# V stored channel by unit, units innermost, in an attention and feed-forward block on one Trainium2 core

## The reference, cut to what matters

```
n = layernorm(x)
q, k, v = n @ Wq, n @ Wk, n @ Wv             # 16 heads of 64 channels
M, Z = memory0, z0                           # per sequence and head
for each segment of 128 rows:                # 4 segments
    att_dot = softmax(mask(q k^T / 8)) @ v
    sq, sk = elu(q) + 1, elu(k) + 1
    att_mem = (sq @ M) / (sq @ Z^T)
    M, Z = M + sk^T @ v, Z + sum(sk)
    out = (gate * att_mem + (1 - gate) * att_dot) @ Wo
x = x + layernorm(out)
x = x + layernorm(ffn(layernorm(x)))         # ffn: three cycles of a small four-layer net
```

## Time and profile before

| | |
|---|---|
| median of three runs | 1286.04 us |
| the profiled execution | 1285.42 us, its span 1283.6 us, mean TensorE clock 0.946 of full |
| TensorE matmuls busy | 1092.2 us, 85% |
| weight loads busy | 761.9 us, 59% |
| VectorE | 876.0 us, 68% |
| ScalarE | 594.8 us, 46% |
| GpSimd | 581.6 us, 45% |
| chain that ended last | TensorE 49%, VectorE 30%, issue 11%, ScalarE 6% |
| 96 stream transposes of `take_x` (L771) | 190.4 us, 7% of the span on the chain |

### The profile page before, as it was taken

One profiled execution on the slowest core, in us unless ns is written; L12 is line 12 of the kernel. 1 busy time (PEld: TensorE's weight loads), 2 busy tenths in 40 slices (PEclk: granted clock), 3 DMA queues, 4 the chain that ended last, 5 costly groups with the idle time before them and its releaser, 6 DMA issues.

```text
span 1283.6 us, 20628 instructions
## 1 busy us (share of the span) xinstructions
PE 1092.2 (85%) x7108; PEld 761.9 (59%) x7172; DVE 876.0 (68%) x1540; ACT 594.8 (46%) x1255; POOL 581.6 (45%) x715
## 2 busy tenths in 40 slices
PE   2798989896989898878889888898989779999992
PEld 1475767664757676657676766576767665433431
DVE  4868686866686868666868686868686654443486
ACT  4354444444454445543535454444444543444453
POOL 2145454544354545444545454545454552222264
PEclk9999999988999989989999999999999888999995
DMA  5000000000000000000000000000000010300033
GB/s 160 21 10 9 10 9 10 10 13 7 10 9 10 9 9 9 9 11 10 9 9 9 9 9 9 9 9 9 9 1 9 2 27 1 139 0 0 1 65 66
DMA packets 14682, 24.02 MB, mean 19 GB/s; under 512 B 5104, under 2 KB 6896, under 8 KB 14064
## 3 DMA queue, kind: packets, MB, share of 16 engines
q1 hardware_dynamic: 14576, 22.63, 5.8%
HBM read 13.97 MB, written 8.65 MB: 18 GB/s over the span
## 4 chain that ended last, share of the span: by engine, by line
PE 49%; DVE 30%; issue 11%; ACT 6%; POOL 2%; DMA 1%; SPq 0%; DVEq 0%; POOLq 0%; ACTq 0%
PE ps L1068 11%; PE ps L1173 9%; DVE arena L771 7%; PE ps L1279 6%; PE ps L1126 5%; DVE arena L868 3%; PE ps L1292 3%; PE ps L1131 3%; PE ps L1113 2%; ACT arena L557 2%; DVE arena L715 2%; DVE arena L781 2%; DVE arena L802 2%; PE ps L1158 2%; DVE arena L785 2%
## 5 line engine op out<-in xcount | busy, mean ns | idle before, releaser
L1068 PE MATMUL ps<-arena 128*128 128x512 f16 x1152 | 273.6, 389 | 6.0 <-DVE arena L747 4.2
L557 ACT ACTIVATE arena<-ps,arena 128x128 f32<-128x128 f32 x512 | 138.9, 383 | 223.5 <-DVE arena L792 223.2
L771 DVE STREAM_TRANSPOSE arena<-ps 128x1024 f32<-128x1024 f32 x96 | 190.4, 1985 | 43.3 <-PE ps L1068 43.3
L1068 PEld LDWEIGHTS ps<-arena 128*128 128x128 f16 x1152 | 113.7, 100 | 131.5 <-issue 17.9
L402 POOL TENSOR_TENSOR arena<-arena 128x256 f32<-128x256 f32 x128 | 92.9, 726 | 164.0 <-DVE arena L802 164.0
L1126 PEld LDWEIGHTS ps<-arena 128*128 128x128 f32 x1024 | 134.2, 200 | 25.2 <-issue 16.9
L1126 PE MATMUL ps<-arena 128*128 128x65 f32 x1024 | 136.8, 278 | 12.9 <-DVE arena L802 11.6
L386 POOL TENSOR_TENSOR arena<-arena 128x512 f32<-128x512 f32 x64 | 81.3, 1270 | 124.6 <-ACT arena L550 124.6
L1173 PE MATMUL ps<-arena 128*128 128x256 f32 x544 | 122.0, 382 | 0.3 <-ACT arena L569 0.3
L1173 PEld LDWEIGHTS ps<-arena 128*128 128x128 f32 x544 | 102.0, 190 | 16.0 <-issue 0.8
L372 POOL TENSOR_TENSOR arena<-arena 128x2 f32<-128x2 f32 x50 | 9.7, 195 | 218.2 <-DVE arena L711 218.2
(11 more groups left out here) (109 smaller groups left out, 1937.8 us busy)
## 6 DMA issues: line engine op xcount, KB each, us to landing
x_rows<-arena SPq DMA_DIRECT2D x17, 256.0 KB, 2.0
arena<-in_L_attn_x_dram SPq DMA_DIRECT2D x64, 64.0 KB
arena<-x_rows SPq DMA_DIRECT2D x4, 1024.0 KB, 7.9
out_dram<-arena SPq DMA_DIRECT2D x32, 128.0 KB, 2.9
arena<-in_L_attn_Wq_dram SPq DMA_DIRECT2D x1, 1024.0 KB, 12.9
arena<-in_L_attn_Wk_dram SPq DMA_DIRECT2D x1, 1024.0 KB, 15.0
arena<-in_L_attn_Wv_dram SPq DMA_DIRECT2D x1, 1024.0 KB, 17.1
arena<-in_L_attn_Wo_dram SPq DMA_DIRECT2D x1, 1024.0 KB, 13.0
```

Source lines behind the costliest of these rows:

```text
L557: last = act.activation(Pr[:, par, j, :], s_bank[:, par, j * P:(j + 1) * P], ACT.Exp, bias=negm[:, par, j:j + 1])
L771: dve.transpose(dst[:, d0:d0 + 32, :], bank.rearrange("p w (d c) -> p d w c", c=C)).then_inc(x_free, 1)
L1068: last = pe.matmul(bank[:, w, :], xc[:, lx, k, w * P:(w + 1) * P], W16[lw][:, k, i, :], start=(n == 0), stop=(n == 5))
```

## The change

V loses its padding and is stored with the channel as the slow index: word `e * 32 + u` in place of `u * 68 + e`. The ones become 32 adjacent words at the end. All users of V follow.

```diff
-VS = DK + 4
...
-        v_pos = [alloc(UNITS * VS)]
+        v_pos = [alloc(UNITS * DV1)]
...
-        v_pos.append(alloc(UNITS * VS))
+        v_pos.append(alloc(UNITS * DV1))
...
-                pool.memset(v_pos[0].rearrange("p (u e) -> p u e", u=UNITS)[:, :, DK:DV1], 1.0).then_inc(init, 1)
+                pool.memset(v_pos[0][:, DK * UNITS:], 1.0).then_inc(init, 1)
...
-                pool.memset(v_pos[1].rearrange("p (u e) -> p u e", u=UNITS)[:, :, DK:DV1], 1.0).then_inc(init, 1)
+                pool.memset(v_pos[1][:, DK * UNITS:], 1.0).then_inc(init, 1)
...
-                    dst = (q_pos, k_pos, v_pos)[i // 2][par].rearrange("p (u e) -> p e u", u=UNITS)
+                    dst = (q_pos, k_pos, v_pos)[i // 2][par].rearrange(
+                        "p (e u) -> p e u" if i >= 4 else "p (u e) -> p e u", u=UNITS)
...
                 def read_out(bp, s, g, half):
...
-                    v = v_pos[s % 2].rearrange("p (u e) -> p u e", u=UNITS)
+                    v = v_pos[s % 2].rearrange("p (e u) -> p u e", u=UNITS)
...
                 def remember(bp, s, g):   (TensorE's)
...
-                    v = v_pos[s % 2].rearrange("p (u e) -> p u e", u=UNITS)
+                    v = v_pos[s % 2].rearrange("p (e u) -> p u e", u=UNITS)
```

## The result

The changed kernel takes 1297.33 us (median of four runs, 1296.86 to 1299.14) against 1286.23 us for the kernel before: ratio 1.0089, 95% interval 1.0076 to 1.0103. It is 11 us slower where no change was forecast. The time lies inside the stated range of 1271 to 1320, but outside the 1280 to 1292 that the forecast's own case allowed. The profiled execution has a span of 1295.4 us.

The account below looks back on a forecast made before the run. The prediction took the TensorE-VectorE hand-offs as the bound, TensorE being fuller. 1285.42 - 12.3 (transposes) + 12 (stepping reads) = 1285.1, with 0.6 for the median 1285.7 us; stated range 1271 to 1320.

Parts of the forecast that it names:

- the forecast's own case: Whole kernel: transposes' gain and TensorE's cost nearly cancel, 1285.7 us, own range 1280 to 1292, chance 0.48.
- U0b: Second half of remember(0), before read_out(1, 1): taken as hidden while VectorE is late, within 0.05 us a step.
- U1: remember(1), after read_out(1, 1): taken as hidden while VectorE is late, within the same 0.05 us a step.
- The gain: V's transposes in take_x (L771): 0.82 us saved each, one a step on the chain, 12.3 us.
- ScalarE's slow rate: TensorE's stepping read of V, given ScalarE's rate for a stepping read: about 1.7 ns a column.
- Rival 1: TensorE's matmuls on V: the step is hidden altogether, only the gain stands, 1274 us; chance 0.27.
- rival 3: TensorE's matmuls on V: every column is fetched twice, some 1445 us; chance 0.06.
- rival 4: V's transposes don't get faster while TensorE pays as in the forecast, 1298 us; chance 0.07.
- rival 2: TensorE's matmuls on V: the step costs more and TensorE becomes the bound, 1315 us; chance 0.12.
- U2b: Second half of remember(2): on the chain with the read-out behind it, 0.40 us, 4.0 us in all.
- U3: remember(3): 0.79 us more, partly hidden by idle time before the next read-out, 0.48 x 12 = 5.8 us.
- the little at `remember(0)`: Stretch from remember(0) to remember(1): cost mostly hidden by waits, 12 x 0.05 = 0.6 us.

Follow-up runs that it names:

- write_stepped: Changed kernel with V written as before, at a step of 68 words, while TensorE still reads at a step of 32: 1310.58 us.
- adjacent: Changed kernel with both TensorE matmuls reading adjacent words of V (values not those of the unit): 1270.05 us.
- readout_adjacent: Changed kernel with the read-out matmul L1126 reading adjacent words, only L1146 stepping: 1293.06 us.
- u01_adjacent: Changed kernel with adjacent words read only in remember(0) and remember(1), everything else stepping by 32 words: 1286.96 us.
- fill: Changed kernel with read_out(1, 1) run before the second half of remember(0) instead of behind it: 1285.3 us.

## Why the prediction was wrong, step by step

The prices of single instructions were the ones forecast. The step of the sum that failed is the one on `remember(0)`, which had a cost hidden that was not hidden. The prediction names this as its own weak point at its end: wrong with both rates right, if the waits don't hide U0b and U1.

- **The gain: right for a transpose, small in the sum.** V's transposes take 1.24 us for the 1.22 forecast, and a step with an update gains 0.79 us of the 0.82. (The 1.05 ns a word behind the 1.22 come from two different operations, a reduction out of PSUM and batch-norm statistics out of SBUF; that they held for a transpose wasn't shown by any row.) 12.3 us were counted; write_stepped against the changed kernel gives 13, adjacent 16.5. The three steps at the end of a pair show hardly any of it in Y (78.6 to 78.3), and part of the 16.5 lies in X and Z, so that 12.3 came near is in part luck.
- **The rate of the stepping read: right.** 220 and 112 ns for 221 and 110. ScalarE's slow rate was a good guide for TensorE. One reading was off: the 122 ns for L1146 before hold one gap of 202 ns in the middle of the eight, and a record in a running row takes 112, so that the step costs 111 ns and not 99. Where the sum says it costs nothing, at low clock, U1 does: (355.01 - 353.21) / 8 = 225 ns, against 216 in the earlier trace rows. Rival 1 falls with adjacent, rival 3 with the rate, rival 4 with the 1.24 us, though its time, 1298, is by chance the measured one; rival 2 has its dearer step at 24 words, but not at 32.
- **`remember(2)`, `remember(3)` and the read-outs about them: right.** U2b 0.40, U3 0.48 and the read-outs about 0.1, less 0.82, is 0.16 a step; Y of one step went from 20.95 to 21.05. With slow transposes, in write_stepped, the same places cost more (Y is 22.4 in the mean of the eleven steps, against 21.0 in both kernels), so the two halves of the change are not independent there.
- **`remember(0)`: the step that failed.** "U0b, `read_out(1, 1)` and U1 stand while VectorE is the late one [...] I count 0.05." The sum has this as "the little at `remember(0)`", 12 x 0.05 = 0.6 us. It was 1.0 us a step, 11 us in all: X went from 11.13 to 12.12 us in the mean. I had compared VectorE's time with the end of U1a alone. But three things stand in a row behind L731: U0b (0.40 later), the read-out behind it (0.07 more), which VectorE takes with `divide(1, 1)`, and both halves of U1 (0.79 more). The read-out had almost no slack. In the kernel before its records end near 348.88 + 0.67 = 349.55, and VectorE comes for it at 349.79:

```profile
348.04 1.00 PE L1126 MATMUL ps<-arena 128*128 128x65 f32 x8
348.88 0.67 PE L1131 MATMUL ps<-arena 128*128 128x130 f32 x4
```

```profile
349.79 0.21 DVE L799 RECIPROCAL arena<-ps 128x8 f32<-128x8 f32 x1
```

  Rival 2 of the prediction adds this stretch up as a whole, less 0.8 us; with the forecast's own rates that gives 0.40 + 0.05 + 0.79 - 0.8 = 0.44 us a step, near what was measured. The one step of the changed kernel that ran all this at full clock shows what that costs by itself, in the VectorE timeline:

```profile
868.53 1.20 DVE L820 TENSOR_TENSOR arena<-ps,arena 64x130 f32<-64x130 f32 x4
870.00 0.21 DVE L799 RECIPROCAL arena<-ps 128x8 f32<-128x8 f32 x1 [0.27 <-PE ps L1131]
870.24 0.69 DVE L802 TENSOR_TENSOR arena<-ps,arena 128x512 f32<-128x512 f32 x1
870.89 0.59 DVE L820 TENSOR_TENSOR arena<-ps,arena 64x130 f32<-64x130 f32 x2
871.79 0.59 DVE L820 TENSOR_TENSOR arena<-ps,arena 64x130 f32<-64x130 f32 x2 [0.30 <-PE ps L1146]
```

  0.27 + 0.30: X is 11.28 there against 10.73 in the full-clock steps before, 0.55 us, or 6 us over eleven steps. Other kernels that step in U0 and U1 agree: write_stepped has two steps at full clock, with X 11.29 and 11.28, and readout_adjacent one, with 11.26.
- **The clock in that stretch: not weighed.** The other 5 us are the distance of X's mean from that full-clock value, which grew from 11.13 - 10.74 = 0.39 to 12.12 - 11.28 = 0.84 us a step, times eleven. I had counted low clock there as a saving, since a stepping column costs nothing more at it. But the read-out between U0b and U1 takes longer at it: its eight L1126 and four L1131 take 353.21 - 350.88 = 2.33 us there, and 1.34 us at full clock in the kernel before (349.38 - 348.04). The windows of the profile show which level it was in this one step, first the kernel before, then the changed one:

```profile
347.49:350.36 2.87, 2.87 (x24) 2.85 (x25) 2.66 (x8) 2.17 (x8) 1.15 (x2) 1.00 0.23 86
```

```profile
350.88:355.01 4.13, 4.13 (x21) 4.05 (x20) 2.63 (x9) 1.79 (x7) 0.19 (x1) 0.59 0.00 0
```

  In the kernel before five of the eleven steps have X within 0.02 us of 10.75, in the changed one not one is under 11.28. From U0b to the end of U1 the granted clock is full in five of the eleven steps before and in one of the changed. TensorE had waited about 2 us before this stretch in both (2.18 and 1.84 us). Why the lower level falls on it more often after the change is open; in u01_adjacent it falls on all eleven, without the price of U0 and U1. The mean clock of the whole execution hardly moved, 0.946 to 0.941. The share of 6 and 5 us is worked out from single profiled executions and is an estimate.
- **The independent proof** is fill: every matmul reads the same words as in the changed kernel, only the order changes, X falls to 10.91 and the whole 12 us come back. A cost was on the path there not because TensorE was full, but because it came behind a wait for VectorE, with VectorE waiting for its end. The clock moved with the order: in fill the stretch has full clock in five of the eleven steps (in the changed kernel in one), and the mean of the execution is 0.955. So fill gives both parts back together and doesn't part them; it shows that with this order the lower clock no longer lengthens X (10.93 at a granted 0.72).

The Trainium skill's "SBUF — State Buffer", in the box on cachelines of "Door 1", has lines of 16 bytes, and each access to a new line pays. The trace agrees: a step of 2 words costs next to nothing, 4 words the full price, and of the odd pairs only those across a border of 16 bytes pay (120 against 210 ns a record). The Trainium skill's "Vector Engine (DVE) Microarchitecture Reference", section 5.2, states for VectorE that runs of two words have to start on an 8-byte boundary. TensorE doesn't follow that here, since odd pairs within 16 bytes are free. The same section of the Trainium skill has 2.5 ns for VectorE at a step of 24 words. TensorE's trace has the same, 2.5 ns.

## What to carry to other kernels

To make a strided VectorE write contiguous by handing the step to TensorE's moving operand moves a price of 0.8 ns a word ((2.04 - 1.24) us / 1024) to one of about 0.9 ns a column ((223 - 112) ns / 130), and TensorE reads the same words more than once. Look for an order in which TensorE reads two adjacent words of the same 16 bytes, as taking two units channel by channel did here. Slack has to be read at each place for everything that stands behind the late release, not for the first that VectorE asks for: three operations each a little longer, between a wait for VectorE and a wait of VectorE, add up (1.26 us here), and what exceeds VectorE's own lateness is paid (0.55 us at full clock, more at low clock). The first thing to try there is the order: work that doesn't need the release belongs in front of it.

## What the runs showed of the hardware that wasn't expected

- A float32 matmul with a stepping moving operand takes 1.7 to 1.8 ns a column from a step of 4 words on (220 to 237 ns a record of 130 columns), 1.4 at a step of 3 (176 ns), and 2.5 at a step of 24 words (320 ns). A step of 2 words costs nearly nothing (117 against 112 ns). Pairs of words cost nothing if both lie in the same 16 bytes, on an odd start too (120 ns), and the full price if they lie across the border (210 ns).
- In PSUM neither TensorE's writes with a hop of 65 words (120 ns a record, 122 without) nor VectorE's reads with a step of 2 words (288 ns, 287 without) cost anything that shows.
- A stream transpose of 1024 words takes 1.24 us into a contiguous run and 2.04 with a step of 68 words.
